# Second cross-attention of a perceiver block: queries prepared in two halves, spreading put ahead of a key rotation on POOL

## What is computed

```python
q = (x @ Wq.T).reshape(B, T, H, D).transpose(0, 2, 1, 3)
k = (context @ Wk.T).reshape(B, S, H, D).transpose(0, 2, 1, 3)
v = (context @ Wv.T).reshape(B, S, H, D).transpose(0, 2, 1, 3)
q = rms_norm(q, q_norm_w)
k = rms_norm(k, k_norm_w)
q_cos, q_sin = precompute_freqs_1d(D, T, Q_THETA)
k_cos, k_sin = precompute_freqs_1d(D, S, K_THETA)
q = apply_rope(q, q_cos, q_sin)
k = apply_rope(k, k_cos, k_sin)
attn = jax.nn.softmax(jnp.einsum('bhtd,bhsd->bhts', q, k) * D ** (-0.5), axis=-1)
out = jnp.einsum('bhts,bhsd->bhtd', attn, v)
```

## Time and profile before

| | us |
|---|---|
| median of 3 runs | 1150.31 (1144.82 to 1152.75) |
| the profiled execution | 1141.98 |
| its span, first to last instruction | 1140.1 |
| PE busy in the span | 919.8 (81%) |
| DVE busy | 504.1 (44%) |
| ACT busy | 465.6 (41%) |
| POOL busy | 322.3 (28%) |

### The profile page before, as it was taken

How to read it: one execution, slowest core, us unless ns; L and a number is a source line. 1 busy time by engine, 2 the same in 40 slices (tenths; PEclk the granted TensorE clock), 3 DMA queues, 4 the chain that set the end, 5 groups by cost and what they waited for, 6 DMA issues and landing times.

```text
span 1140.1 us, 23919 instructions
## 1 busy us (share of the span) xinstructions
PE 919.8 (81%) x8634; PEld 744.6 (65%) x8634; DVE 504.1 (44%) x1454; ACT 465.6 (41%) x1370; POOL 322.3 (28%) x374
## 2 busy tenths in 40 slices
PE   5899999979785399999945399999986860799980
PEld 3677777644564199999934277777755650699970
DVE  3556656530564211111165567777765552122222
ACT  2677677623232033333233176777765630111100
POOL 2211121001100500000072467787861414000004
PEclk9999999979897599999977599999998865899995
DMA  8111126000000688888341011111000004699943
GB/s 253 62 40 39 38 72 216 3 1 0 1 1 1 237 309 326 323 323 329 132 153 37 1 39 39 39 39 37 0 2 2 2 1 168 221 336 336 336 164 106
DMA packets 50561, 135.75 MB, mean 119 GB/s; under 512 B 16168, under 2 KB 37552, under 8 KB 44464
## 3 DMA queue, kind: packets, MB, share of 16 engines
q1 hardware_dynamic: 47408, 126.28, 31.0%
q0 software_dynamic: 3072, 8.39, 2.2%
HBM read 117.35 MB, written 17.30 MB: 118 GB/s over the span
## 4 chain that ended last, share of the span: by engine, by line
PE 70%; DVE 15%; POOL 5%; issue 4%; ACT 2%; SPq 2%; DMA 2%; DVEq 0%; POOLq 0%; ACTq 0%
PE lower L1010 15%; PE upper L1019 10%; PE upper L592 9%; PE upper L614 8%; PE upper L650 5%; PE lower L636 3%; PE upper L667 3%; POOL xslot L1992 3%; PE upper L792 2%; DVE x L1834 1%; PE upper L687 1%; PE upper L603 1%; PE lower L535 1%; POOL arena L1998 1%; PE upper L671 1%
## 5 line engine op out<-in xcount | busy, mean ns | idle before, releaser
L1010 PEld LDWEIGHTS lower<-arena 128*128 128x128 f32 x1472 | 174.7, 195 | 6.1 <-DVE arena L1800 3.9
L1010 PE MATMUL lower<-arena 128*128 128x128 f32 x1472 | 175.5, 278 | 2.7 <-DVE arena L1800 2.7
L1019 PE MATMUL upper<-arena 128*128 128x256 f32 x552 | 126.4, 379 | 0.0
L1998 POOL DMA_INDIRECT arena<-yslot,slot x32 | 30.6, 957 | 322.9 <-DMA yslot<-arena 313.7
L614 PE MATMUL upper<-wkv,arena 128*128 128x256 f32 x512 | 121.4, 380 | 0.0
L1019 PEld LDWEIGHTS upper<-arena 128*128 128x128 f32 x552 | 101.5, 190 | 12.0
L614 PEld LDWEIGHTS upper<-wkv,arena 128*128 128x128 f32 x512 | 94.8, 191 | 11.6
L1341 ACT ACTIVATE arena<-lower,arena 128x128 f32<-128x128 f32 x184 | 52.5, 369 | 106.0 <-PE lower L1010 105.9
L650 PE MATMUL upper<-const,arena 128*128 128x128 f32 x512 | 80.2, 280 | 6.8 <-ACT arena L1149 6.2
L650 PEld LDWEIGHTS upper<-const,arena 128*128 128x128 f32 x512 | 59.7, 143 | 28.2 <-issue 12.4
L592 PE MATMUL upper<-wkv,arena 128*128 128x256 f32 x256 | 71.1, 412 | 4.8 <-DMA arena<-in_ctxT_dram 4.5
(11 more groups left out here) (230 smaller groups left out, 1624.6 us busy)
## 6 DMA issues: line engine op xcount, KB each, us to landing
arena<-in_ew_dram SPq DMA_DIRECT2D x23, 2048.0 KB, 7.2
arena<-in_ew_dram SPq DMA_DIRECT2D x23, 1536.0 KB, 6.2
arena<-in_ctxT_dram SPq DMA_DIRECT2D x16, 1028.0 KB, 5.2
xslot<-zero SPq DMA_DIRECT2D x2, 2944.0 KB, 15.2
arena<-xslot SPq DMA_DIRECT2D x46, 128.0 KB, 5.8
yslot<-arena SPq DMA_DIRECT2D x46, 128.0 KB, 6.1
const<-in_const_dram SPq DMA_DIRECT2D x1, 1152.0 KB, 7.7
x<-in_x_dram SPq DMA_DIRECT2D x1, 1024.0 KB, 5.6
```

The source lines that it names most:

```text
L1010: ins = mm(bank[1 + half][:, i * P:i * P + P], ew[k][:, at:at + P], exT[k % 2][:, c, :], start=(c == 0), stop=(c == KC - 1))
L1019: ins = mm(bank[4 + k % 2][:, 0:D], eh[k % 2][:, i, :], ew[k][:, at:at + D], start=(i == 0), stop=(i == nh - 1))
L1998: G.indirect_dma_start(out=eyg[t][i], out_offset=None, in_=yslot[l], in_offset=at(i, t))\
```

## The change

DVE's query work becomes a function with a half (tiles 0 to 3 or 4 to 7) and a step (1: sum and root; 2: the product with the root and the first rope product; 3: the other rope products and the sum). The first half runs where all eight tiles did, and waits for four projected tiles only; the second half's steps 1, 2 and 3 stand at the end of slots 1, 2 and 3. PE transposes four tiles ahead of slot -1, and the other four two at a time in slots 4 and 5, each ahead of a values product and into the free half of its PSUM bank; ACT copies each from there ahead of the values' copy. On DVE the key normalization of batch 1 moves from slot -2 to the end of the early slots, ahead of the experts' sum. On POOL the difference and the rotation of slot -2 move up behind the early slots, and the first spread moves ahead of slot -1. POOL waits in slot 7 until all queries have been copied.

```diff
@@ PE, values of a slot
+                    if l == 1 and isinstance(n, int) and n == 1 and j < 2:
+
+                        if j == 0 and w == 0:
+                            pe.wait_ge(q["qrope"], 2)
+                        for c in range(KC):
+                            nc.tensor.transpose(bank[6 + w][:, D + c * P:D + c * P + P],
+                                                xn[:, 4 + 2 * j + w, c * P:c * P + P], ident)
@@ PE, ahead of slot -1
                     pe.wait_ge(q["qrope"], 1)
-                    for b in range(4):
+                    for b in range(2):
...
-                    pe.wait_ge(q["qtc"], 4)
+                    pe.wait_ge(q["qtc"], 2)
@@ ACT, values of a slot
+                    if l == 1 and isinstance(n, int) and n == 1 and j < 2:
+                        t = 4 + 2 * j + w
+                        A(qT[:, :, t * P:t * P + P], bank[6 + w][:, D:2 * D].rearrange("p (c q) -> p c q", c=KC), copy)\
+                            .then_inc(q["qtc"], 1)
@@ DVE
+                def queries(half, step):
...
+                    q0, q1 = flat(xn)[:, mine4], flat(outT)[:, mine4]
+                    q2 = flat(outT if half else qT)[:, 0:4 * D]
+                    if step == 1:
+                        dve.wait_ge(q["qc"], 4 * half + 4)
+                        mine(V.tensor_reduce(qss[:, 0:nh], h3(q1), AX_X, ALU.add))
+                        inv_root(qr[:, 0:nh], qss[:, 0:nh], nh, mine)
+                    elif step == 2:
+                        mine(V.tensor_tensor(h3(q0), h3(q0), qr[:, 0:nh].unsqueeze(2).to_broadcast([P, nh, HD]), ALU.mult))
+                        dve.wait_ge(q["rw"], 1)
+                        mine(V.tensor_tensor(h3(q1), h3(q0), bc(rope_q[:, 0:HD], HD), ALU.mult))
+                    else:
+                        if half:
+                            dve.wait_ge(q["qrope"], 1)
+                        V.tensor_tensor(h3(q2)[:, :, 0:8], h3(q0)[:, :, 8:16], bc(rope_q[:, HD:HD + 8], 8), ALU.mult)
+                        mine(V.tensor_tensor(h3(q2)[:, :, 8:16], h3(q0)[:, :, 0:8], bc(rope_q[:, HD + 8:2 * HD], 8), ALU.mult))
+                        V.tensor_tensor(q0, q1, q2, ALU.add).then_inc(q["qrope"], 1)
...
-                    norm(n, k, j, it)
+                    if not (isinstance(n, int) and n == -1 and j == QB - 2):
+                        norm(n, k, j, it)
...
                     sums(n, k, j, it)
+                    if isinstance(n, int) and n == 0 and j > 0:
+                        queries(1, j)
@@ DVE, end of the early slots
                     slots(dve, slot, -KEYS_AHEAD[l], 1 - EARLY)
+
+                    norm(-1, 1, QB - 2, None)
                     return
...
+                    for step in range(1, 4):
+                        queries(0, step)
                     slots(dve, slot, 1 - EARLY)
@@ POOL
+                        if isinstance(n, int) and n == 1 and j == QB - 1:
+
+                            pool.wait_ge(q["qtc"], 6)
...
                     slots(pool, slot, -KEYS_AHEAD[l], -TURN_AHEAD)
+                    differ(-1, 1, QB - 2, None)
+                    rotate(-1, 1, QB - 2, None)
                     pool.wait_ge(q["lastkeys"], 7)
-                    slots(pool, slot, -TURN_AHEAD, 0)
-                    pool.wait_ge(q["qtc"], 4)
+                    last_column(-1, 1, QB - 2, None)
+                    pool.wait_ge(q["qtc"], 2)
                 for c in range(KC):
                     spread(0, 0, c)
+                if l == 1:
+                    slots(pool, slot, -1, 0)
                 slots(pool, slot, 0)
```

21 lines of the change are left out of this document (6 added, 15 removed).

## The result

The changed kernel takes 1140.24 us in the median of 13 runs (1135.93 to 1145.98), the kernel before, in 13 runs, 1150.85: a ratio of 0.992, with an interval of 0.9896 to 0.9943. The prediction was 1143.0 within 1134 to 1152, and a change of at most 1% either way was its likeliest case (0.71). The total came out nearly as forecast, yet the two profiled executions seem to say something else, so the profile has to be read with care.

What follows compares the result with a forecast made beforehand. TensorE, busy 81% of the span, was taken to bound, standing still before the first scores behind DVE's query chain and POOL's rotations. -15.4 us (start) + 8.1 (second half) took 1141.98 to 1134.7; the median's 8.3 offset gave 1143.0, range 1134 to 1152.

## What to carry to other kernels

One profile is one execution: before costing a stretch by it, compare its time with the median, and if it is quick, ask which wait of the stretch may be missing from it; here a second profile of the unchanged kernel explained the most. Products and root steps that are moved on DVE to fill its idle time beside a busy POOL are paid twice, by their own overrun (1.9 us here) and by the turns that the two engines take (4.7); the same widths as sums paid only the first, and two other placings of the work still paid more than half of the toll. When a chain's start is worth microseconds, look one stage further up as well: a gain as large as the change's, 7.4 us of the stretch (287.09 to 279.70) and 9 of the time, lay in the issue order of gathers that the change never touched.

## What the runs showed that was not expected

- ScalarE stood still for 7 to 10 us in its copies, with no releaser in the program, in eleven of the twelve traces in which sixteen gathers were issued beside them; in one of the eleven the profile names issue and PE for the same two gaps (4.61 and 3.14 us). With the gathers halved, or half of them issued later, in one trace each, it did not. The mechanism is open.
- Gathers issued on POOL did not lengthen DVE's merges (0.99 us a pair), POOL's elementwise work did (up to 2.57).
- Where two engines take turns, each one's duration contains a wait for the other: a copy of two columns on POOL, 0.19 us, is shown at 1.18.
- With the moved transposes but not the second half's work, PE had more to do and a shorter wait ahead of slot 6 (1.24 us in place of 2.14): the granted clock stayed at 1.00, and the slot took 7.36 us in place of 8.87.
